# A recommender tower with a cross network: another spread of the gathers, two weight pieces later, other SBUF addresses, a last layer in four tiles

## The reference

```python
e = jnp.stack([tbl_f[ids[:, f]] for f in range(39)], axis=1)      # 512 x 39 x 16
xk, outs = e, []
for W in (f0, f1, f2):                                            # f0: 39*39 x 128, f1, f2: 128*39 x 128
    z = jnp.einsum('bfd,bgd->bfgd', e, xk).reshape(b, f * g, d)
    xk = jnp.einsum('bpd,pm->bmd', z, W)
    outs.append(xk)
z = jnp.sum(jnp.concatenate(outs, axis=1), axis=-1)               # 512 x 384
h = jnp.concatenate([z, dense_ctx], axis=1)                       # dense_ctx: 512 x 16
h = jnp.maximum(h @ W_top1 + b_top1, 0.0)
h = jnp.maximum(h @ W_top2 + b_top2, 0.0)
y = h @ W_top3
```

## Time and profile before

| | |
|---|---|
| median of 3 runs | 643.72 us (643.5 to 644.06) |
| the profiled execution | 648.03 us |
| its span, first to last instruction | 646.4 us |
| outside the span | 1.6 us |
| TensorE busy | 616.8 us, 95% of the span |
| VectorE, ScalarE, GpSimd busy | 540.2, 358.0 and 516.3 us |
| mean granted clock of TensorE | 0.997 of full |

### The profile page before, as it was taken

One profiled execution on the slowest core, in us unless ns is written; L12 is line 12 of the kernel. 1 busy time (PEld: TensorE's weight loads), 2 busy tenths in 40 slices (PEclk: granted clock), 3 DMA queues, 4 the chain that ended last, 5 costly groups with the idle time before them and its releaser, 6 DMA issues.

```text
span 646.4 us, 11120 instructions
## 1 busy us (share of the span) xinstructions
PE 616.8 (95%) x3096; PEld 467.0 (72%) x3096; DVE 540.2 (84%) x1656; ACT 358.0 (55%) x1200; POOL 516.3 (80%) x486
## 2 busy tenths in 40 slices
PE   0699899999999999999999999999999999999998
PEld 0376667677788777777788777777788777778873
DVE  5299889999995889999995889999995889988911
ACT  4245457656554565656563565656573565657612
POOL 6479898999995989999995999999995996766620
PEclk9999999999999999999999999999999999999999
DMA  7451527451410505041320505032330504100000
GB/s 235 111 124 46 130 40 221 173 134 27 112 48 11 150 3 158 3 112 50 90 72 9 152 3 140 22 92 70 65 96 3 144 18 114 42 1 2 1 2 0
DMA packets 63101, 48.86 MB, mean 76 GB/s; under 512 B 38916, under 2 KB 44428, under 8 KB 62912
## 3 DMA queue, kind: packets, MB, share of 16 engines
q1 hardware_dynamic: 56392, 42.89, 23.2%
q0 software_dynamic: 5120, 1.32, 3.0%
q10 hardware_dynamic: 1528, 3.95, 1.7%
HBM read 46.20 MB, written 1.94 MB: 74 GB/s over the span
## 4 chain that ended last, share of the span: by engine, by line
PE 70%; POOL 17%; issue 4%; DVE 4%; DMA 2%; ACT 1%; another core or an unknown queue 1%; SPq 1%; POOLq 0%; DVEq 0%; ACTq 0%
PE strip L994 16%; PE strip L998 15%; PE strip L995 15%; PE acc L954 11%; POOL added L586 5%; POOL found L576 5%; PE acc L1025 4%; POOL added L593 4%; DVE scaled L724 3%; PE strip L1012 2%; POOL added L596 2%; POOL x_t L602 1%; PE strip L1025 1%; PE strip L1096 1%; PE strip L1039 1%
## 5 line engine op out<-in xcount | busy, mean ns | idle before, releaser
L724 DVE SCALAR_TENSOR_TENSOR scaled<-strip,x_t,scaled 128x128 f32<-128x128 f32 x1216 | 331.2, 343 | 28.1 <-PE strip L998 27.7
L994 PE MATMUL strip<-w_hi,x_hi 128*128 128x512 f32 (+1 forms) x640 | 290.9, 454 | 0.7 <-ACT x_hi L809 0.7
L998 PE MATMUL strip<-w_hi,x_lo 128*128 128x512 f32 (+1 forms) x640 | 249.4, 390 | 0.0
L995 PE MATMUL strip<-w_lo,x_hi 128*128 128x512 f32 (+1 forms) x640 | 249.0, 389 | 0.0
L586 POOL TENSOR_TENSOR added<-added,product 128x512 f32<-128x512 f32 x128 | 170.2, 1329 | 51.8 <-ACT product L865 46.2
L865 ACT ACTIVATE product<-strip,x_t 128x128 f32<-128x128 f32 x512 | 147.0, 374 | 113.8 <-PE strip L998 110.9
L576 POOL DMA_INDIRECT found<-in_tables,rows x160 | 168.5, 1053 | 34.2 <-issue 13.7
L994 PEld LDWEIGHTS strip<-w_hi,x_hi 128*128 128x128 f32 x640 | 120.6, 188 | 45.4 <-issue 15.2
L995 PEld LDWEIGHTS strip<-w_lo,x_hi 128*128 128x128 f32 x640 | 120.8, 189 | 42.8 <-issue 21.8
L998 PEld LDWEIGHTS strip<-w_hi,x_lo 128*128 128x128 f32 x640 | 120.3, 188 | 26.0
L655 DVE TENSOR_TENSOR z<-shifted,x_thrice 128x512 f32<-128x512 f32 (+2 forms) x105 | 103.2, 988 | 9.6 <-issue 7.9
(11 more groups left out here) (67 smaller groups left out, 233.9 us busy)
## 6 DMA issues: line engine op xcount, KB each, us to landing
shifted<-x_fields SPq DMA_DIRECT2D x91, 234.0 KB
x_thrice<-x_fields SPq DMA_DIRECT2D x29, 234.0 KB
shifted_last<-x_fields SPq DMA_DIRECT2D x14, 234.0 KB
found<-in_tables,rows POOLq DMA_INDIRECT x160
w<-in_L_rec_f SPq DMA_DIRECT2D x1, 2496.0 KB
g_sum<-in_L_rec_f ACTq DMA_DIRECT2D x4, 512.0 KB
shifted<-x_fields SPq DMA_DIRECT2D x56, 22.0 KB
shifted<-x_half_fields SPq DMA_DIRECT2D x10, 117.0 KB
```

Source lines behind the costliest of these rows:

```text
L724: dve.scalar_tensor_tensor(into, strip[:, slot_of_strip(q) % Y_BANKS, j, :], x0_t[:, c % 2, s, f:f + 1], onto, ALU.mult, ALU.add).then_inc ...
L994: pe.matmul(into, x1_hi[:, c % 2, columns], hi, start=True, stop=False)
L995: pe.matmul(into, x1_hi[:, c % 2, columns], lo, start=False, stop=False)
L998: pe.matmul(into, x1_lo[:, c % 2, columns], hi, start=False, stop=True).then_inc(strip_ready, 1)
```

## The change

1. **Gathers.** A table `GATHERS_IN` says how many gathers each sub has. Chunks 4 and 8 have 16 (4 in each sub), chunk 12 has 14, chunks 5 to 7 and 9 to 11 have 8 (2 in each sub), chunk 0 has 14 and not 16, chunks 2 and 3 have 9. Chunks 1 and 13 keep 10 and 4. At the start GpSimd issues all five gathers of half 0 before it adds the first rows for the other chunks.
2. **Start.** ACT loads three pieces of layer 1's weights at the start and the other two only when the sixth `shifted` tile of half 0 has landed. Their high parts come behind ACT's `high_x1(0)`, their low parts behind VectorE's `sum_x1(0)`. SP issues all seven `shifted` tiles of half 0. TensorE's matmuls for the dense features wait for the gathers of half 0 and no longer for the write.
3. **SBUF.** A spare buffer and another order of the allocations put all large buffers at multiples of 512 bytes. In the program before, `w1_hi` and `w1_lo` began 192 bytes past such a multiple, `x0_thrice` to `x1_lo` 416 bytes past one, and `first` to `out2` 384 bytes past one. `found`, `rows`, `ids` and `x0_t` stay off such multiples.
4. **Last layer.** Each of its two matmuls is cut into four, one for each 128 examples, whose results go to PSUM rows 0, 32, 64 and 96 by `tile_position`. ACT copies 97 x 128, and SP sends four rows.

```diff
-T0_BY_SP = 3
+Y_TILE = P // QUARTERS
+Y_ROWS = Y_TILE * (QUARTERS - 1) + 1
-AHEAD = 2 * GATHERS + 6
 AHEAD_OF_X1 = 2 * GATHERS - 4
-GATHERS_IN_SUB = 3
-GATHERS_IN_FIRST_SUBS = 4
+GATHERS_IN = [(4, 4, 3, 3), (3, 3, 2, 2), (3, 2, 2, 2), (3, 2, 2, 2),
+              (4, 4, 4, 4), (2, 2, 2, 2), (2, 2, 2, 2), (2, 2, 2, 2),
+              (4, 4, 4, 4), (2, 2, 2, 2), (2, 2, 2, 2), (2, 2, 2, 2),
+              (4, 4, 3, 3), (2, 2, 0, 0), (0, 0, 0, 0), (0, 0, 0, 0)]
+W1_EARLY = 3
...
+        sb("spare", [P, 3 * P // 4])
         ident = sb("ident", [P, P])
-        mask = sb("mask", [P, TILE_B])
         w0 = sb("w0", [P, T0, MAPS])
...
-        y = first[0:1, 0, :, :].rearrange("p j m -> p (j m)")
+        y = first[0:Y_ROWS, 0, 0, :]
...
-        y_bank = last_banks[3][0:1, :]
+        y_bank = last_banks[3][0:Y_ROWS, 0:P]
...
-                for t in range(tiles_of(i) if i else T0_BY_SP):
+                for t in range(tiles_of(i)):
...
-            sp.dma_start(a["out"].rearrange("b o -> o b"), y).then_inc(y_out, 16)
+            sp.dma_start(a["out"].rearrange("(t b) o -> t (b o)", t=QUARTERS), y[0:Y_ROWS:Y_TILE, :]).then_inc(y_out, 16)
...
             pool.wait_ge(rows_ready, 1)
-            gather(0)
+            for n in range(HALF_GATHERS):
+                gather(n)
             add_first_rows(1, CHUNKS, CHUNKS)
             pool.wait_ge(rows_ready, 2)
-            for n in range(1, AHEAD_OF_X1):
+            for n in range(HALF_GATHERS, AHEAD_OF_X1):
                 gather(n)
...
-                    upto = min(GATHERS * c + min(GATHERS_IN_SUB * (s + 1), GATHERS) + AHEAD, CHUNKS * GATHERS)
-                    left = min(GATHERS_IN_SUB if c else GATHERS_IN_FIRST_SUBS, upto - next_one)
+                    left = GATHERS_IN[c][s]
...
-            for i in range(W1_PIECES - 1):
+            for i in range(W1_EARLY):
                 low_w1(i)
             for t in range(T0):
                 products0(0, t)
-            low_w1(W1_PIECES - 1)
             low_x1(0)
             sum_x1(0)
+            for i in range(W1_EARLY, W1_PIECES):
+                low_w1(i)
...
+            for i in range(W1_EARLY):
+                load_w1(i)
             act.wait_ge(dense_turned, 1)
             act.wait_ge(dense_zeroed, 2)
             act.copy(dense_t[0:D, :], dense_bank).then_inc(dense_kept, 1)
-            for i in range(W1_PIECES):
-                act.wait_ge(w1_in[i], 16)
-                act.copy(w1_hi[:, w1_fields(i), :], w1_raw[:, w1_fields(i), :]).then_inc(w1_hi_ready, 1)
-            act.wait_ge(written_half[0], 16 * WRITES)
-            for t in range(T0_BY_SP, T0):
-                act.dma_start(shifted[0:ROWS, t, columns_of(0)],
-                              shifted_fields(0, PER_TILE * t, PER_TILE, 1)).then_inc(shifted_in[t], 16)
+            for i in range(W1_EARLY):
+                high_w1(i)
...
+            act.wait_ge(shifted_in[T0 - 2], 16)
+            for i in range(W1_EARLY, W1_PIECES):
+                load_w1(i)
             keep_x0_t(0)
             high_x1(0)
+            for i in range(W1_EARLY, W1_PIECES):
+                high_w1(i)
...
-            pe.wait_ge(written_half[0], 16 * WRITES)
+            pe.wait_ge(gathered_half[0], 16 * HALF_GATHERS)
...
-                last = pe.matmul(y_bank, wt3[:, k:k + 1], h2[:, k, :], start=(k == 0), stop=(k == H2 // P - 1))
+                for t in range(QUARTERS):
+                    last = pe.matmul(y_bank[Y_TILE * t:Y_TILE * t + 1, :], wt3[:, k:k + 1], h2[:, k, P * t:P * t + P],
+                                     start=(k == 0), stop=(k == H2 // P - 1), tile_position=(0, Y_TILE * t))
```

More of the change, by code:

```diff
@@ L262, in build_program @@
         w0_stack = sb("w0_stack", [ROWS, MAPS], F32R)
-        roles = sb("roles_sb", [ROWS, PER_TILE])
         w1_hi = sb("w1_hi", [P, FIELDS, MAPS], F32R)
@@ L266, in build_program @@
         w2 = sb("w2", [P, FIELDS, MAPS])
-        ids = sb("ids_sb", [P, CHUNKS + 2, GATHERS], I32)
-        rows = sb("rows", [P, CHUNKS, GATHERS], I32)
-        found = sb("found", [P, E_SLOTS, GATHERS, D])
         x0_thrice = sb("x0_thrice", [P, 2, N])
@@ L283, in build_program @@
         x1_lo = sb("x1_lo", [MAPS, 2, N], F32R)
-        x0_t = sb("x0_t", [P, 2, SUBS, FIELDS])
-        x0_diag = sb("x0_diag", [P, SUBS, TILE_B, FG])
         first = sb("first", [P, 2, PER_STRIP, MAPS])
@@ L296, in build_program @@
         out2 = sb("out2", [MAPS, BATCH])
-        dense = sb("dense_sb", [P, QUARTERS, D])
         dense_t = sb("dense_t", [P, BATCH])
-        bias1 = sb("bias1", [P, H1 // P])
-        bias2 = sb("bias2", [P, H2 // P])
         wt1 = sb("wt1", [P, 3, H1])
@@ L305, in build_program @@
         wt2 = sb("wt2", [P, H1 // P, H2])
+        mask = sb("mask", [P, TILE_B])
+        roles = sb("roles_sb", [ROWS, PER_TILE])
+        ids = sb("ids_sb", [P, CHUNKS + 2, GATHERS], I32)
+        rows = sb("rows", [P, CHUNKS, GATHERS], I32)
+        found = sb("found", [P, E_SLOTS, GATHERS, D])
+        x0_t = sb("x0_t", [P, 2, SUBS, FIELDS])
+        x0_diag = sb("x0_diag", [P, SUBS, TILE_B, FG])
+        dense = sb("dense_sb", [P, QUARTERS, D])
+        bias1 = sb("bias1", [P, H1 // P])
+        bias2 = sb("bias2", [P, H2 // P])
         wt3 = sb("wt3", [P, H2 // P])
@@ L872, in _, with load_w1, high_w1 @@
             act.dma_start(w0_mirror, a["w0_lower"]).then_inc(w0_in, 16)
-            for i in range(W1_PIECES):
+            def load_w1(i):
                 act.dma_start(w1_raw[:, w1_fields(i), :], a["L0_rec_f1"][:, w1_fields(i), :]).then_inc(w1_in[i], 16)
+            def high_w1(i):
+                act.wait_ge(w1_in[i], 16)
+                act.copy(w1_hi[:, w1_fields(i), :], w1_raw[:, w1_fields(i), :]).then_inc(w1_hi_ready, 1)
+            for i in range(W1_EARLY):
+                load_w1(i)
             act.wait_ge(dense_turned, 1)
```

## The result

| | before | the change |
|---|---|---|
| median | 643.89 us (643.5 to 644.34, 4 runs) | 648.17 us (647.37 to 649.08, 4 runs) |
| ratio | 1 | 1.0061, interval 1.0049 to 1.0073 |

The change makes the kernel 4.3 us slower; the forecast was 1.1 us slower, 644.9. It is where the second rival stood with 648.3.

The account below looks back on a forecast made before the run. TensorE sets the time, with GpSimd slightly later in chunks with ten gathers. Start -0.65, middle +2.54, addresses 0 and last layer -0.75 sum to +1.14 us on 643.72: 644.9 us, range 638.0 to 648.5.

Parts of the forecast that it names:

- second rival: Start and middle: late weights, and half clock behind new waits in chunks 5 and 9; 648.3 us, chance 0.15.
- line 1012 waits 1.9 us: Chunks 5 and 9: three more gathers ahead of the last `x_t` outrun 1.5 us of slack; range 1.8 to 2.3.
- another 0.95 us: Line 1012 one chunk later, chunks 6 and 10: ten gathers between last `x_t`s make TensorE wait 0.95 us again.
- +0.65: Chunk 13: two more gathers in chunk 12, 2.2 us, against 1.5 us of slack cost 0.65 us.
- +2.54 us: Middle chunks: the gather table's savings and new waits together make the kernel 2.54 us slower.
- 1.12 us: Chunks 2 and 3: with nine gathers instead of ten, both waits for GpSimd go, saving 1.12 us.
- upper bound: Line 1012 between 116.30 and 480.81 us: a table removing every wait for `x_t` would gain 3.9 us.
- -1.26 and -0.4: Chunk 0's fewer gathers: one gather less before the wait at 78.07 saves 1.26 us, less half clock behind it 0.4.
- +1.0: Start: ACT's first strip waits for the last late low part of the weights, 1.0 us later; range -0.5 to +2.5.
- Forecast 0: Strip matmuls: buffers at multiples of 512 bytes change nothing; bounds -38 and +1 us.
- Forecast -0.75: End of kernel: last layer's matmuls in four tiles and a narrower copy save 0.75 us; range -1.1 to -0.4.
- late weights and a half clock: Rival for start and middle: weights at their late bound, clock falls behind chunks 5 and 9's waits; 648.3 us, chance 0.15.

Follow-up runs that it names:

- gathers_alone: The kernel before with only the change's table of gathers, without the five gathers issued first: 648.8 us, ratio 1.0085.
- before_again: The kernel before, unchanged, timed and profiled once more: 643.22 us, ratio 1.000; its profile spans 642.7 us.
- gathers_in_first_sub: The kernel before with the change's gathers per chunk, but 7 in the first sub of chunks 4, 8 and 12: ratio 0.9963.
- start_alone: The kernel before with only the change's edits of the start, including the five gathers issued first: 645.43 us, ratio 1.0036.

## Why the prediction was right, and where not

**The middle: the mechanism was right, and its size short by the clock.** The step "line 1012 waits 1.9 us" in chunks 5 and 9 was measured at 2.05 in gathers_alone and 2.34 in the change. GpSimd's last `x_t` of chunk 4 ended 3.6 us later than before, counted from layer 2's end, where 3.4 was forecast. The step "another 0.95 us" one chunk later holds only where the clock stays up. In the change line 1012 waits 0.18 us in chunk 6, behind a fall, and 0.74 us in chunk 10, behind the wait without one:

```profile
264.41 1.13 PE L1028 MATMUL strip<-x_diag,x_t 32*128 32x80 f32 x32 [0.18 <-POOL x_t L609]
...
413.10 1.13 PE L1028 MATMUL strip<-x_diag,x_t 32*128 32x80 f32 x32 [0.74 <-POOL x_t L609]
```

A fall gives GpSimd 1.6 us to catch up. The sum had nothing for the clock; the rival had 1.6 us each, less something for that second wait, and 1.61 were measured. Chunk 13 was forecast at +0.65 and measured at +0.91. As a whole the term was +2.54 us. From chunk 2's first strip to the end gathers_alone takes 544.35 us and before_again 536.40, which is +7.95: 3.2 of the difference are two falls of the clock, and 2.0 are small waits that before_again didn't have and that the sum gave back. gathers_in_first_sub shows that the place in the chunk is the cause.

**Chunks 2 and 3** were to gain 1.12 us, from line 1012 of chunk 2 to that of chunk 4. They gained 0.67 in gathers_alone (69.11 us against 69.78 in before_again). The wait at the head of that stretch, for which the sum had no change, grew from 1.41 to 1.66 us. In the change it was 1.83, the clock fell behind it, and chunk 2 took 37.51 us where before_again has 36.02.

**The upper bound** of 3.9 us was from one execution, and left out the waits at 78.07 and 116.30. In before_again the later small waits are 2.0 us less, so it would be about 1.9 there.

**Chunk 0's gathers.** The terms were -1.26 and -0.4. Measured in gathers_alone: -3.6 us in chunk 1. Three quarters of the wait went (2.05 to 0.51) and the fall of the clock with it.

**The start: the step that failed.** The write of half 0 was forecast at 12.9 and came at 12.73, the sixth tile at 24.6 and came at about 24.3, ACT's first strip at 32.3 and came at 31.69. The two loads were guessed at 4 to 5 us and landed 3.9 and 4.8 us after their issue. All this was right and didn't decide. The late loads I had followed only up to the weights' own arrival, and not for the transfers of half 1 that they stand beside: 1 MB of weights at 24 to 29.5 us and the write of half 1 are under way at the same time. I had named the gathers as what the loads might share the engines with, for the weights' sake alone. The stall of 3.06 us and the 1.6 us of half clock behind it outweigh the earlier first strip: in start_alone chunk 2 starts 0.8 us later than in before_again (107.15 against 106.33), though chunk 1 had no fall of the clock there, and the time is 2.3 us longer (0.36%). For the start without chunk 0's gathers +1.0 was forecast, with +2.5 as its end: the size fits the range, the way it comes about doesn't.

**Addresses.** Forecast 0, measured -0.8 us. The reasoning from two offsets was not sound: durations at 192 and at 416 bytes are alike, but neither says what a start at a multiple of 512 takes. The effect is 0.003 to 0.008 us for a matmul, and in some strips only, and not the 0.02 of the bound, and part of it turns into waits for GpSimd.

**Last layer.** Forecast -0.75, measured -0.65. From ACT's bias to SP's issue it takes 2.30 us and not 3.35, which is 0.3 more than I had, and SP's issue 0.60 and not 0.25, for which I had 0. From ACT's bias to the copy it is 2.01 us and not 2.74, 0.73 saved where 0.45 was forecast: the four tiles of one `k` take 0.40 us from first start to last end. The reading from which I took their overlap was wrong. Line 1012 is 16 matmuls of two passes, not 32 with 64 passes, and its tiles lie in different rows of the array (`tile_position=(TILE_ROWS * t, 0)`), not in different columns.

**The sum.** Alone the parts cost 0.85, 0.36, -0.13 and -0.10%, together 0.98%; the change costs 0.61%. The difference of 0.37%, 2.4 us, isn't settled. It doesn't hang on the table: start, addresses and last layer alone add up to +0.13%, and together, in without_gathers, they measured -0.28%, 0.41% less. Whether they gain more together, or ratios of different series don't add up so closely, isn't shown.

So the forecast's place and sign for the table were right. For the size, 1.1 us of 4.3, it had the clock at nothing and the harm of the late weights in the wrong place, and chunk 0's gathers gained more than it had, which hid part of that. That the range held is in part luck: it was wide enough for rivals of both signs. Most of what the forecast lacked is in the rival "late weights and a half clock", whose account was right in the clock and wrong in how the weights do harm. That it stood at 648.3 is luck too, since its 1.0 us for later weights did not come about.

Three versions beat before most: gathers_in_first_sub, before with another table (ratio 0.9963, 2.4 us faster), without_gathers, the change without its table (0.9972, 1.8 us), and start_w1_early, the new start with all weights early (0.9978, 1.4 us). They were not run together.

## What to carry to other kernels

Work that is put into an engine's idle time belongs ahead of the instruction that ends the idle time. Behind it, it delays the next hand-over, however idle the engine is on average in that stretch.

A load that is put off doesn't go away: look at what else is in the DMA engines when it comes, and above all at short transfers on which a chain waits.

A wait of TensorE has a second price in the clock, and a way to save one wait of 2 us may be worth 3.6. And before a step is thinned out, both of its limits have to be read: who waits for the engine, and who waits for what the step fetches.

## What the runs showed of the hardware that was not expected

**The clock behind a wait.** Over all profiles here, TensorE waited between 1.2 and 1.71 us at line 1012 eleven times, and the granted clock stayed at 1.00 behind each. It waited between 1.76 and 2.36 us fifteen times, and the clock fell to half in eleven of these, ten times for some 3 us and once, in without_gathers, for some 7. Where it can be read alone, in chunk 5 of gathers_alone and between chunks 5 and 9 of the change, that costs 1.6 us. The four without a fall were of 1.90, 1.91, 2.12 and 2.34 us, so the length of the wait alone doesn't settle it. The Trainium skill ("TensorE: Matmul & The Clock Gate", section "Why this matters for your kernels") has the fall behind an idle TensorE, and the runs agree that it comes. The waits that brought it here, 1.76 to 2.36 us, are shorter than the gaps that the section warns of, and the measurement decides.

**A matmul's pace and the address of its data.** 512 columns in split float32 take 0.225 to 0.23 us in the undisturbed strips when weights and data start at multiples of 512 bytes, and 0.233 at 192 and 416 bytes past one. Whether it is the weights' or the data's address wasn't separated.

**A write beside a large load.** The same write landed 1.1 to 2.6 us after its last issue where no weights were on the way, and 3.9 to 4.5 us beside 1 MB of them.
